# A sequence layer and an eight-expert layer on one core: routing steps reordered, copies and casts moved between engines, zeros multiplied in the setup

## What is computed

```python
lam = exp(-exp(nu_log) + 1j * exp(theta_log)); gamma = sqrt(1 - abs(lam) ** 2)
states = lru_scan(lam, einsum('bld,nd->bln', x, gamma[:, None] * (B_re + 1j * B_im)))
y = einsum('bln,mn->blm', states, C_re + 1j * C_im).real + einsum('bld,md->blm', x, D_mat)
x = layernorm(x + x + sigmoid(res_logit) * (gelu(y @ W1, tanh) @ W2))
probs = softmax(x @ Wg); weights, indices = top_k(probs, 2)
for e in range(8):                              # cw: the two weights, zero elsewhere
    out += (gelu(x @ FW1[e] + fb1[e], exact) @ FW2[e] + fb2[e]) * cw[:, e:e+1]
x = layernorm(x + out)
```

## Time and profile before

| | |
|---|---|
| Median of 3 runs | 329.77 us (328.82 to 332.23) |
| The profiled execution | 328.72 us |
| its span, first to last instruction | 326.1 us |
| mean granted TensorE clock | 0.934 |
| busy share PE, DVE, ACT, POOL | 84%, 70%, 67%, 63% |

### The profile page before, as it was taken

How to read it: one execution, slowest core, us unless ns; L and a number is a source line. 1 busy time by engine, 2 the same in 40 slices (tenths; PEclk the granted TensorE clock), 3 DMA queues, 4 the chain that set the end, 5 groups by cost and what they waited for, 6 DMA issues and landing times.

```text
span 326.1 us, 5241 instructions
## 1 busy us (share of the span) xinstructions
PE 274.4 (84%) x1287; PEld 214.9 (66%) x1287; DVE 228.6 (70%) x729; ACT 219.0 (67%) x474; POOL 204.4 (63%) x241
## 2 busy tenths in 40 slices
PE   1689999699779985887969999999999999992910
PEld 1335664446465653776959899999999999940400
DVE  3833599839584875966987789888888888700880
ACT  2516464765454474679967899999999999910480
POOL 3405347067887877740677787777777777771680
PEclk9999999989969999599998999999999999996975
DMA  4994100001111115325774556556556555315951
GB/s 87 319 331 115 35 1 0 0 0 36 41 58 41 49 41 174 130 99 165 236 268 140 200 192 216 190 182 221 202 178 221 195 167 204 113 56 206 357 170 57
DMA packets 31365, 46.39 MB, mean 142 GB/s; under 512 B 5096, under 2 KB 23024, under 8 KB 31336
## 3 DMA queue, kind: packets, MB, share of 16 engines
q1 hardware_dynamic: 25620, 35.97, 33.6%
q0 software_dynamic: 4832, 9.97, 9.3%
q10 hardware_dynamic: 884, 0.12, 0.2%
HBM read 16.99 MB, written 13.86 MB: 95 GB/s over the span
## 4 chain that ended last, share of the span: by engine, by line
POOL 39%; PE 22%; issue 14%; DVE 13%; ACT 5%; DMA 3%; DVEq 1%; ACTq 0%; POOLq 0%; SPq 0%
POOL results_d L460 28%; POOL slots_d L454 8%; PE bank L1092 4%; PE bank L1040 3%; PE bank L1071 2%; PE bank L1041 2%; PE bank L1042 2%; PE bank L1072 2%; PE bank L1073 2%; PE bank L1182 1%; PE bank L1057 1%; POOL early L485 1%; DMA logs<-in_L_attn_nu_log_dram 1%; PE bank L1029 1%; DMA rows<-results_d 1%
## 5 line engine op out<-in xcount | busy, mean ns | idle before, releaser
L460 POOL DMA_INDIRECT results_d<-work,dest x87 | 92.1, 1058 | 26.5 <-issue 26.5
L454 POOL DMA_INDIRECT slots_d<-rows,slot_i x64 | 65.6, 1026 | 31.3 <-issue 18.2
L940 DVE TENSOR_TENSOR h_l<-h,h_h 128x384 fp32r<-128x384 f32 x116 | 65.0, 560 | 15.4 <-ACT h_h L605 12.7
L600 ACT ACTIVATE h<-bank,buse 128x384 f32<-128x384 f32 x116 | 67.9, 586 | 8.1 <-DVE h_l L940 5.0
L1040 PE MATMUL bank<-h_h,wuse 128*128 128x384 f32 x116 | 45.0, 388 | 5.0 <-DVE h_l L940 5.0
L1040 PE MATMUL bank<-xbt_h,wuse 128*128 128x384 f32 x116 | 41.2, 355 | 0.7 <-ACT h L600 0.4
L1041 PE MATMUL bank<-xbt_l,wuse 128*128 128x384 f32 x116 | 40.5, 349 | 0.0
L1042 PE MATMUL bank<-xbt_h,wuse 128*128 128x384 f32 x116 | 40.4, 348 | 0.0
L1041 PE MATMUL bank<-h_l,wuse 128*128 128x384 f32 x116 | 39.6, 342 | 0.0
L1042 PE MATMUL bank<-h_h,wuse 128*128 128x384 f32 x116 | 39.6, 341 | 0.0
L531 ACT ACTIVATE h<-bank 128x512 f32<-128x512 f32 x32 | 18.8, 597 | 22.7 <-PE bank L1042 22.1
(11 more groups left out here) (198 smaller groups left out, 549.0 us busy)
## 6 DMA issues: line engine op xcount, KB each, us to landing
...
```

The lines of the kernel that those rows point to most:

```text
L454: pool.indirect_dma_start(out=slots_d, out_offset=bass.IndirectOffsetOnAxis(ap=slot_i[:, k, i:i + 1], axis=0), in_=rows[:, k, i, :], in_of ...
L460: pool.indirect_dma_start(out=results_d, out_offset=bass.IndirectOffsetOnAxis(ap=dest[:, SQ * g + q:SQ * g + q + 1], axis=0), in_=yo[:, g ...
L600: act.activation(h32[:, b % 2, 0:SLOTS], H_PS[b % 2][:, 0:SLOTS], ACT.Gelu, bias=buse[:, k, b:b + 1]).then_inc(sm["gelu_b"], 1)
L940: dve.tensor_tensor(ht_l[b], h32[:, b % 2, 0:SLOTS], ht_h[b].bitcast(F32), ALU.subtract).then_inc(sm["hbl_ready"], 1)
```

## The change

Ten edits, named here for later:

- **a. PE setup.** POOL zeroes the tile `zeros` first of all; PE multiplies it six times (`keep_awake(6)`, 128x256 products into a bank not yet used) before its first transpose, and twice more within `outputs(0)`. `inputs(0)` now stands ahead of `x_transposed(1)`.
- **b. outputs(c).** The product of x comes first, and the products of `qc` and `qs` wait each for their own copy.
- **c. ACT and DVE setup.** The Sin table is loaded at ACT's start; `gam` is made ahead of the wait for the Sin; `y_low(0)` moves behind four small DVE instructions that PE's chunk 0 also waits for.
- **d. ACT's casts.** ACT casts 3 pieces ahead of `y_high(0)`, 4 in chunk 0, 4 in chunk 1 and none later.
- **e. POOL's casts.** POOL casts the last five pieces itself, and starts `weights_low` when `y_low(0)` is done; the `norm` stand behind pieces 7, 13 and 16.
- **f. dispatch.** `norm(3)` stands behind 10 of the 16 DMAs of dispatch 0 instead of 8.
- **g. Row copies.** The second copy of the rows of chunks 0 to 5 is a DMA issued by SP, not an ACT copy.
- **h. Exponents first.** In routing chunks DVE does the exponents and `offsets` ahead of the counts; `offsets` stands ahead of `y_low` everywhere.
- **i. first_weights** moves ahead of `stats(6)` in the last chunk (its second weight copy stays behind `pre_a`), and needs `route_ready` 1 instead of 2.
- **j. Hand-over on PE.** `xt(0, 0)` stands ahead of `r_transposed(7)`, and `logits(7)` between the first two hidden parts of tile 0.

```diff
+ROWS_BY_SP = 6
+CASTS_BY_ACT = (3, 4, 4)
...
         def _(pool):
+            pool.memset(zeros[:], 0.0).then_inc(sm["zero_ready"], 1)
             pool.memset(ident[:], 0.0).then_inc(sm["pool_link"], 1)
...
                 e, a = divmod(n, 2)
+                if n >= sum(CASTS_BY_ACT):
+                    pool.wait_ge(fw_loaded[e], 32)
+                    pool.tensor_copy(fw_part(e, a, 0), fw_part(e, a, 1).bitcast(F32)).then_inc(sm["fw_hi"], 1)
                 pool.wait_ge(sm["fw_hi"], n + 1)
...
+            pool.wait_ge(sm["y_lo"], 1)
             for n in range(NFW):
-                if n in (4, 8, 12):
-                    norm(n // 4 - 1)
+                if n in (7, 13):
+                    norm((7, 13).index(n))
                 weights_low(n)
+            norm(2)
             for g in range(NG - 1):
-                dispatch(g, 0, 4)
+                at = (5, 4, 4)[g]
+                dispatch(g, 0, at)
                 norm(2 * g + 3)
-                dispatch(g, 4, 8)
+                dispatch(g, at, 8)
...
+            for c in range(ROWS_BY_SP):
+                sp.wait_ge(sm["row0_ready"], c + 1)
+                sp.dma_start(rows[:, 1, QT * c:QT * (c + 1), 0:D], rows[:, 0, QT * c:QT * (c + 1), 0:D]).then_inc(row1_ready[group_of(c)], 16)
...
+            act.preload_act_table_set("trig_and_small")
             act.dma_start(logs[:, 2:3], bass.AP(tensor=res_logit.tensor, offset=0, ap=[[0, P], [1, 1]])).then_inc(sm["res_loaded"], 16)
...
             act.preload_act_table_set("gelu_apprx_tanh_and_others")
+            for n in range(CASTS_BY_ACT[0]):
+                weights_high(n)
             y_high(0)
...
                 if ended is not None:
                     route_weights(ended)
+                if c == NCH - 1:
+                    first_weights()
                 if c >= 1:
                     stats(c - 1)
                     aggregate(c - 1)
...
                     route_choice(g, 1)
+                    route_exponents(g)
+                if c >= 1:
+                    offsets(c - 1)
+                if g is not None:
                     route_hits(g)
                 if c + 1 < NCH:
                     y_low(c + 1)
-                if c >= 1:
-                    offsets(c - 1)
-                if g is not None:
-                    route_exponents(g)
...
+                for _ in range(n):
+                    mm(R_PS[:, 0:256], zeros[:, 0:P], zeros[:, 0:256], start=True, stop=True)
+
+            keep_awake(6)
...
                 wait(pe, sm["y_lo"], c)
+                mm(Y_PS[:], dt, xt32[:, c % 3, :], start=True, stop=False)
+                if c == 0:
+                    keep_awake(2)
+                pe.wait_ge(sm["q_ready"], 2 * c + 1)
+                mm(Y_PS[:], wcs[:, 0, :], qc, start=False, stop=False)
                 pe.wait_ge(sm["q_ready"], 2 * c + 2)
-                mm(Y_PS[:], wcs[:, 0, :], qc, start=True, stop=False)
-                mm(Y_PS[:], wcs[:, 1, :], qs, start=False, stop=False)
-                mm(Y_PS[:], dt, xt32[:, c % 3, :], start=False, stop=True).then_inc(sm["y_ready"], 1)
+                mm(Y_PS[:], wcs[:, 1, :], qs, start=False, stop=True).then_inc(sm["y_ready"], 1)
...
                 chunk(c)
+            xt(0, 0)
             r_transposed(NCH - 1)
-            xt(0, 0)
-            logits(NCH - 1)
             pe.wait_ge(sm["w1use_ready"], 1)
             pe.wait_ge(sm["xb_lo"], 1)
             hidden(0, 0, 0)
+            logits(NCH - 1)
             hidden(0, 0, 1)
```

39 lines of the change are left out of this document (21 added, 18 removed).

## The result

The changed kernel takes 0.9672 of the time of the kernel before (95% interval 0.9619 to 0.9725), with a median of 329.29 us before in these runs. Its median is 318.37 us (317.6, 318.37 and 321.57); one disturbed execution of it, 357.85 us, and the disturbed ones of other kernels are left out of every ratio and median here. The profiled execution is the shortest, 317.60 us, with a span of 315.8 and a mean granted clock of 0.937. The forecast was 322.0, in a range of 313 to 327.5.

The account below looks back on a forecast made before the run. It saw POOL's DMA queue and the PE/ACT/DVE loop end the expert stage nearly together, so gains come earlier; terms summing to -7.8 us took the profiled 328.72 to 320.9, plus 1.05 for the median: 322.0, range 313 to 327.5.

Parts of the forecast that it names:

- The frame: Expert stage, unedited: shifts as a whole, one to one with what the chunk stage wins or the hand-over loses.
- B: Rival: POOL hinders DVE less, ACT hides the hand-over, chunk 4 is not held up: 316 us, chance 0.18.
- A: The sum of the terms as it stands: 322 us, between 318.5 and 325.5, chance 0.50.
- D: Rival: POOL's cast is as slow as its subtraction, +2.1 us in chunk 2: 324 us, chance 0.12.
- E: Rival: slower, DMAs lengthen and delay norms 3, 5, 7; gain gone from +0.30 us a DMA, 337 to 338 at +0.6; chance 0.10.
- Setup: Before chunk 0: products wait less and run at full clock, chunk 0 starts at 17.5 instead of 22.86: -5.3 us.
- Rival C: Setup: zero products don't keep the clock up through the wait, gain 2.3 instead of 5.3: 325 us, chance 0.10.
- Chunks 0 and 1: POOL's subtractions, begun earlier, each block a two-input DVE step beside scan and turning back: +0.9 us.
- POOL beside DVE: Chunk 2: POOL's casts (0.55 us each) and subtractions block two-input DVE steps, so counts come late: +1.5 us.
- Chunk 3: Gelu comes sooner after the counts, leaving 0.5 us of PE waiting and 0.4 of low clock: 12.3 for 16.20, -3.9 us.
- Chunks 4 and 5: Chunk 4: norm(3) behind ten DMAs delays counts, +1.4 us; chunk 5: earlier offsets and gelu, -4.8 us.
- Hand-over: Last chunk into expert stage: first_weights delays the first expert product by 1.4 us, logits(7) costs 1.0: +2.4 us.

Follow-up runs that it names:

- norms_inside: all_casts_early with norms 2, 4, 6 behind the first two DMAs of the following dispatch, norms 3, 5 behind eight, norm(7) behind ten, PE's hand-over order as before: 314.84 us, ratio 0.9562.
- no_zeros: Changed kernel without the eight products of zeros on PE: 320.31 us, ratio 0.9730.
- outputs_back: Changed kernel with outputs(c) as before, waiting for both copies, then the products of qc, qs and x; zeros kept: 324.07 us, ratio 0.9852.
- all_casts_early: Changed kernel with all casts on ACT by the end of chunk 1, POOL only subtracting, norm(0) behind nine pieces, norm(1) and norm(2) behind all: 315.31 us, ratio 0.9562.
- logits_and_norm7: Changed kernel with PE's hand-over order as before and norm(7) behind four DMAs of dispatch 2 instead of eight: 323.09 us, ratio 0.9806.
- weights_back: Changed kernel with the weight split as before: ACT casts four pieces in each of chunks 0 to 3, POOL only subtracts, norms behind pieces 4, 8, 12: 323.81 us, ratio 0.9824.
- pe_handover_back: Changed kernel with PE's hand-over order as before: r_transposed(7), xt(0, 0), logits(7), then the hidden parts of tile 0: 318.63 us, ratio 0.9645.
- first_weights_back: Changed kernel with first_weights behind offsets(6) in the last chunk, as before: 317.67 us, ratio 0.9623.

## Why the prediction was right, and where it was not

**The frame held.** It said that the expert stage moves as a block. From the first DMA of the last dispatch to the last write-back it is 138.17 us before, 137.93 after, and between 137.3 and 140.2 in all fourteen profiles, whatever was changed ahead; in each of them POOL issues the 103 DMAs of that block without a gap over 0.32 us. So the time falls when the last dispatch starts earlier. What the prediction did not say is that this start hangs not on DVE's stream alone: POOL's earlier dispatches hold it too, through the load of tile 2. PE waits 1.27 for that load before, 1.24 after, and 5.88 and 7.13 in two runs with a shorter hand-over. In the runs that removed a wait another took its place; that the load of tile 2 is what costs the time is not shown, since norms_inside is without that wait and gains nothing clear.

**The rivals.** 318.4 lies nearer to B's 316 than to A's 322, and just below A's own range. But of B's conditions only one came, a chunk 4 that is not held up; chunk 2 and the hand-over cost what A said or more. D falls with the cast of 0.61, E with the pace of the DMAs (137.93 over 102 is 1.352 each, 1.355 before). E had the right place: the counts come 0.75 us before PE wants them in chunk 4, and there is no more slack than that.

**Setup: right in size, the cause shown in part.** 17.42 for 17.5. The sum split it into order and clock; no_zeros and outputs_back show that the full pace needs both. In outputs_back the second copy is there at 14.54 instead of 15.42, so the 0.9 allowed for the Sin table came as well; no run undoes part c alone. Rival C was priced at 3; without the zeros 1.6 is lost.

**Chunks 0 and 1: +0.60 for +0.9.** Chunk 0's other length, 11.76, would have made it +1.7, so the small error is luck.

**POOL beside DVE: right in kind, 0.9 too small in chunk 2.** The cast was 0.61 for 0.55. What was mis-sized is where the last three pieces begin: `norm(1)` ended 6.9 after the start of chunk 2, not about 6.1, because two casts and two subtractions still stood beside the turning back (two steps in 2.77, where they take 1.28 alone). all_casts_early shows the whole price of POOL's pieces in chunk 2 as 3.0.

**Chunk 3: right in total, 0.5 short, with other parts.** PE waits for nothing in it, where 0.5 was allowed; the low clock costs about 1.4 (12.79 less 11.4) instead of 0.4. The low clock now stands behind chunk 2's wait of 2.89, of which the sum took no price into chunk 3. Without that wait, in all_casts_early, chunk 3 takes 11.94 at a clock of 1.00; but logits_and_norm7 has the wait and 1.00 as well, with 12.53 and a wait of 0.56 for the gelu, as summed.

**Chunks 4 and 5: the mechanism was right, the place of one result was not.** The step took 1.4 us a DMA from dispatch 0 of before. Beside a chunk 3 it was 1.30 (62.55 to 75.57, ten of them); in weights_back, where dispatch 0 starts with chunk 4 again, it is 1.37. With that, and with chunk 4 starting 0.9 later than summed, `norm(3)` ended 9.0 after its start instead of 11.2; the counts came 1.2 behind it, as summed, but at 10.3, just ahead of the 11.01 at which PE wants them. So the 1.4 was not paid, and the offsets stood 2.5 ahead of chunk 5 instead of 1.1. There the wait for the gelu fell to 0.34 instead of 1.6, and the 1.0 allowed for the low clock was not paid either (1.00). These two chunks, 3.45 us, are more than the whole error of the sum, 2.5; 0.9 of the shift in `norm(3)` comes from chunks 2 and 3, which were longer than summed, so part of this gain is the error of other terms. weights_back shows the tipping point that the text named: with dispatch 0 starting 5.3 later against chunk 4, that chunk takes 18.37.

**Hand-over: the sum was right (+2.4 for +2.4), its parts not.** The first product came only 0.64 later, though `nmr(6)` came 2.25 later: before, `x_high` had waited 1.68 for PE, and that slack took most of it. Behind the first product 1.80 was lost instead of 1.0, and the last dispatch stands 27.76 behind it instead of 25.99, which the text had named as a sign of being wrong. It is not the logits alone, as summed: pe_handover_back, without part j, has 27.74. Worked out from the two rows, the lower clock is worth some 1.1 us of it (27.76 x 0.21 less 25.99 x 0.18), an estimate. So the +2.4 is partly luck, and how its second part comes about is not shown. The two causes named are there (first_weights_back: 2.25 at `nmr(6)`; 1.43 for the logits), but neither gives time back alone.
